# The same instructions in new fixed orders: five engine queues and the PSUM bank table of a two-layer transformer kernel laid out again

## The reference

```
x = layernorm(x + attention0(x))          # q, k, v, out without bias
x = layernorm(x + down0(silu(gate0(x) * gs) * (up0(x) * us)) * ds)      # 704 wide
x = layernorm(x + attention1(x))          # q, k, v, out with bias
x = layernorm(x + down1(silu(up1(x)) * gate1(x)))   # 1024 wide, weights made ternary
```

## Time and profile before

| | us |
|---|---|
| median of three runs | 256.35 (256.03 to 258.0) |
| the profiled execution, whole time | 255.42 |
| its span | 253.5 |
| PE, DVE busy | 240.6 (95%), 204.3 (81%) |
| ACT, POOL busy | 161.4 (64%), 167.1 (66%) |

### The profile page before, as it was taken

The page is one execution under the profiler, slowest core; times in us unless marked ns, Lnnn a source line. Parts: engine busy times, 40 slices in busy tenths (PEclk is TensorE's granted clock), DMA queues, the critical chain, the costliest instruction groups (busy, mean ns, idle before and its releaser), DMA issues.

```text
span 253.5 us, 6724 instructions
## 1 busy us (share of the span) xinstructions
PE 240.6 (95%) x2398; PEld 216.3 (85%) x2398; DVE 204.3 (81%) x599; ACT 161.4 (64%) x290; POOL 167.1 (66%) x218
## 2 busy tenths in 40 slices
PE   8998989999999999999999898998999999999991
PEld 8997967877789989989999897765788888999990
DVE  2477976999776876889999998998999975767664
ACT  4682465469889979627444567848788484555551
...
GB/s 164 277 193 203 216 175 241 152 120 79 76 98 109 109 129 119 85 145 144 187 85 189 3 122 189 31 153 145 0 45 3 4 3 0 3 35 8 3 0 124
DMA packets 23312, 26.39 MB, mean 104 GB/s; under 512 B 3184, under 2 KB 18288, under 8 KB 23280
## 3 DMA queue, kind: packets, MB, share of 16 engines
...
## 4 chain that ended last, share of the span: by engine, by line
PE 71%; POOL 6%; DVE 5%; DMA 5%; ACT 5%; issue 4%; SPq 2%; POOLq 0%; ACTq 0%
PE psum L566 9%; PE psum L567 8%; PE psum L568 8%; PE psum L686 6%; PE psum L661 5%; PE psum L741 5%; PE psum L742 5%; DMA k_stack<-k_part 3%; PE psum L629 3%; PE psum L689 2%; PE psum L633 2%; PE psum L664 2%; POOL hidden L1253 2%; PE psum L775 2%; PE psum L638 2%
## 5 line engine op out<-in xcount | busy, mean ns | idle before, releaser
L857 ACT ACTIVATE probs<-psum 128x768 f32<-128x768 f32 x64 | 49.1, 809 | 11.9 <-PE psum L667 5.9
L1253 POOL TENSOR_TENSOR hidden<-hf,hidden 128x512 fp32r<-128x512 f32 x24 | 31.6, 1320 | 13.5 <-ACT hidden L899 13.5
L1221 POOL TENSOR_SCALAR_AFFINE_SELECT probs<-probs 128x512 f32<-128x512 f32 x48 | 32.3, 688 | 10.1 <-ACT probs L857 9.7
L1009 DVE TENSOR_REDUCE block_max<-psum 128x6 f32<-128x768 f32 x32 | 28.9, 946 | 6.0 <-PE psum L633 5.9
L661 PE MATMUL psum<-q_stack,k_stack 98*128 98x256 bf16 x128 | 28.6, 274 | 2.1 <-DMA q_stack<-maxT_lo 1.0
L1020 DVE CUSTOM_DVE_ANT_0 masked<-psum,mask 128x256 bf16<-128x256 f32 x64 | 26.7, 418 | 1.6 <-issue 0.9
L1106 DVE SCALAR_TENSOR_TENSOR hf<-th,psum 128x512 f32<-128x512 f32 x28 | 18.9, 677 | 9.8 <-ACT th L888 3.9
L566 PE MATMUL psum<-xT_hi,gu_hi 128*128 128x256 f32 x88 | 25.3, 288 | 0.0
L567 PE MATMUL psum<-xT_lo,gu_hi 128*128 128x256 f32 x88 | 24.9, 283 | 0.0
L568 PE MATMUL psum<-xT_hi,gu_lo 128*128 128x256 f32 x88 | 24.9, 283 | 0.0
L664 PE MATMUL psum<-q_stack,k_stack 98*128 98x128 bf16 x128 | 24.7, 218 | 0.0
...
## 6 DMA issues: line engine op xcount, KB each, us to landing
q_stack<-q_part SPq DMA_DIRECT2D x48, 128.0 KB, 2.7
k_stack<-k_part SPq DMA_DIRECT2D x48, 128.0 KB, 2.4
...
```

Source lines behind the costliest of these rows:

```text
L857: nc.scalar.activation(probs[(n - 1) % 4][:, :, :], place(key)[:, :, 0:T + P], ACT.Exp, scale=SC).then_inc(exp_done, 1)
L1009: nc.vector.tensor_reduce(block_max[b % 2][:, 2 * i:2 * i + 2, 1:4], both(key)[:, :, 0:3 * P].rearrange("p j (c t) -> p j c t", t=P), mybi ...
L1221: pool.affine_select(out=diag, in_=diag, compare_op=ALU.is_ge, fill=0.0, base=0, pattern=[[0, 2], [0, 2], [1, P]], channel_multiplier=-1). ...
L1253: pool.tensor_tensor(hidden[(n - 1) % NHID][1][:, :, :], hf[n % 2][:, :].rearrange("p (a t) -> p a t", a=2), hidden[(n - 1) % NHID][0][:, ...
```

## The change

The program of every engine consists of the same steps with the same code; only the six tables are different. One line of two of them:

```diff
@@ SYNC_STEPS, first line
-    LOAD:001 LOAD:003 QK:000 LOAD:002 QK:001 MID:000-1 LO:000-1 QK:010 MID:010 LO:010 MID:011 QK:011 LO:011 LO:020
+    LOAD:001 LOAD:003 LOAD:002 QK:000 MID:000 QK:001 MID:001 LO:000-1 LO:010 QK:010-1 MID:010-1 LO:011 LO:020-1
@@ TENSOR_STEPS, first line
-    QK:000 XI:010 QK:001 QK:010 XI:020 XI:030 QK:011 QK:020-1 V:000 V:010 S:000-4 QK:030 S:005-7 QK:031 S:010 MX:000
+    QK:000 XI:010 QK:001 QK:010 XI:020 XI:030 QK:011 QK:020-1 V:000 S:000 V:010 S:001-5 QK:030 S:006-7 QK:031 S:010
```

More of the change, by code:

```diff
@@ L101 @@
[L101 to L105, removed]
@@ new lines @@
+    S:000-7 MB:000 QK:030 S:010 MX:000 QK:031 S:011-5 SCALES:000 UT:000 IV:000 S:016-7 S:020 MB:010 S:021 UT:001
+    MX:010 YM:000 IV:001 S:022-7 YM:001 MB:020 YB:000 S:030 PREP0:004-5 MX:020 UT:010 S:031-2 PREP0:006 O:000 S:033
+    IV:010 UT:011 S:034 IV:011 S:035-7 MB:030 YM:010 XT:000 YM:011 UT:020 YB:010 MX:030 GU:000 IV:020 UT:021 YM:020
+    IV:021 YM:021 O:010 YB:020 GU:001-2 UT:030 HL:002 IV:030 O:020 XT:010 D:000 UT:031 IV:031 YM:030-1 TS:100 YB:030
+    GU:010-1 O:030 XT:020 XT:100 TERN:100 GU:012 TERN:101 QK:100 HL:012 TS:101 XT:030 TERN:102 D:010 TERN:103
@@ new lines @@
+    GU:020-1 TERN:104 QK:101 XT:110 TERN:105 GU:022 GU:030 HL:022 QK:110 S:100-1 TERN:106 QK:111 GU:031 S:102-3
+    D:020 S:104-5 GU:032 S:106-7 S:110 XT:120 HL:032 S:111-2 QK:120 MX:100 D:030 S:113 QK:121 CB:100 S:114-6 XT:130
+    TS:102 S:117 TERN:107 QK:130 MX:110 S:120 QK:131 UT:100 S:121-6 UT:101 IV:100 S:127 IV:101 YM:100-1 TERN:108
+    YB:100 UT:110 MX:120 S:130-2 O:100 S:133 UT:111 S:134-6 XT:200 TERN:109 S:137 IV:110-1 YM:110-1 MX:130 YB:110
+    GU:100 UT:120-1 IV:120 GU:101 O:110 IV:121 YM:120 TERN:1010-11 YM:121 UT:130 YB:120 GU:102-3 XT:210 O:120
@@ L139 @@
+    GU:110-1 UT:131 XT:220 IV:130-1 YM:130-1 YB:130 GU:112-3 D:100 O:130 GU:120 D:110 XT:230 GU:121-3 GU:130-3 D:120
+    DT:130-1 NT:130-1
 """
 GPSIMD_STEPS = """
-    SPLIT:000 VONES:000 SPLIT:001 SPLIT:010-1 SPLIT:020-1 SPLIT:030-1 PREP0:000-3 YT:000 PREP0:004-5 LN:000
-    PREP0:006 ST:020-3 PREP1:000 ST:024-7 PREP1:001-2 YT:010 HI:000 ST:030-3 LN:010 YT:020 ST:034 HI:001-2 ST:035-7
-    LN:020 LN:100 YT:030 HI:010 TERN:100 LN:030 TERN:101 HI:011 TERN:102 HI:012 SPLIT:100 TERN:103 LN:110 TERN:104-5
@@ new lines @@
+    PREP0:004-5 LN:000 ST:020-3 PREP0:006 PREP1:000-1 ST:024-7 YT:010 PREP1:002 ST:030-3 LN:010 HI:000 YT:020
+    HI:001-2 ST:034-7 LN:020 LN:100 YT:030 HI:010 TERN:100 LN:030 TERN:101 HI:011-2 TERN:102-3 SPLIT:100 LN:110
+    TERN:104 HI:020 TERN:105 SPLIT:101 HI:021 TERN:106-7 HI:022 HI:030 SPLIT:110-1 LN:120 HI:031 PREP1:003 HI:032
+    LN:130 SPLIT:120-1 ST:100-1 XC:100 XC:110 ST:102-7 TERN:108 SPLIT:130-1 ST:110-5 YT:100 TERN:109 ST:116-7 ST:120
+    LN:200 ST:121-5 TERN:1010 ST:126-7 YT:110 TERN:1011 ST:130-1 HI:100 ST:132-3 XC:120 LN:210 HI:101 YT:120
@@ L150 @@
 SYNC_STEPS = """
-    LOAD:001 LOAD:003 QK:000 LOAD:002 QK:001 MID:000-1 LO:000-1 QK:010 MID:010 LO:010 MID:011 QK:011 LO:011 LO:020
-    RAW:000-1 LOAD:000 MX:000 ML:000 LO:021 QK:020 MID:020-1 QK:021 RAW:002-3 MID:030 QK:030 MX:010 ML:010 MID:031
-    LO:030-1 QK:031 RAW:004-5 ML:020 MX:020 RAW:006-9 MX:030 ML:030 RAW:0010-25 QK:100 RAW:0026-27 MID:100 QK:101
-    MID:101 LO:100-1 RAW:0028-29 QK:110 RAW:0030 LO:110 QK:111 MID:110-1 LO:111 MX:100 ML:100 QK:120-1 MID:120-1
-    LO:120-1 RAW:0031-32 ML:110 MID:130 MX:110 MID:131 QK:130 LO:130 QK:131 LO:131 ML:120 MX:120 RAW:0033-34 MX:130
-    ML:130 LN:300 LN:310 LN:320 LT:130-1
+    LOAD:001 LOAD:003 LOAD:002 QK:000 MID:000 QK:001 MID:001 LO:000-1 LO:010 QK:010-1 MID:010-1 LO:011 LO:020-1
+    RAW:000 LOAD:000 RAW:001 MX:000 ML:000 MID:020-1 QK:020-1 RAW:002-3 QK:030 MID:030-1 MX:010 ML:010 QK:031
+    LO:030-1 RAW:004-6 ML:020 MX:020 RAW:007-10 MX:030 ML:030 RAW:0011-26 MID:100 RAW:0027 LO:100 QK:100-1 MID:101
+    LO:101 RAW:0028-30 QK:110-1 MID:110-1 LO:110-1 QK:120 ML:100 QK:121 MX:100 MID:120-1 LO:120-1 ML:110 RAW:0031
+    MX:110 RAW:0032 QK:130-1 MID:130-1 LO:130-1 ML:120 MX:120 RAW:0033-34 MX:130 ML:130 LN:300 LN:310 LN:320
+    LT:130-1
 """
 BANKS = """
[7 rows of a table removed]
[7 rows of a table added]
 """
```

65 lines of the change are left out of this document (28 added, 37 removed), and 14 rows, old and new, of the table BANKS.

## The result

| | before | after |
|---|---|---|
| median, same chip, four runs each | 256.19 us (255.89 to 258.0) | 259.58 us (257.9 to 260.03) |
| ratio, 95% interval | | 1.015 (1.011 to 1.019) |
| the profiled execution, its span | 255.42, 253.5 | 260.03, 258.1 |
| PE, DVE busy | 240.6, 204.3 | 240.9, 206.8 |

The change makes the kernel slower by 3.4 us, against a forecast of 2.9 us faster.

A forecast was written before the change was run, and what follows sets the result against it. The PE bounds the kernel, held up mostly by late transfers, with DVE a second bound from 124 us. Terms 1.3 + 0.9 + 0.8 - 0.1 = 2.9 us take 255.42 to 252.5, median 253.4 us; range 251.3 to 256.4.

The forecast's parts named there:

- Start: To 44 us: earlier copies and loads on SP, S:014 ahead of ST:000; gain 1.3 us, ends 0.3 and 1.7.
- 0.65 us of SP's queue: Start: LOAD:002 ahead of QK:000 on SP makes every later copy come 0.65 us earlier.
- 2.4 to land: Start: batch 0's last copy lands 2.4 us after its issue, so S:000 can start between 18 and 19.2.
- rival 2: SP's order is worth nothing; only the moved S step and POOL gain, 1.5 us: 254.9 us, chance 0.08.
- POOL's hidden part: 108 to 124 us: HI:012 ahead of TERN:102 ends D:012's wait; gain 0.9 us, ends 0 and 1.1.
- Layer 1's attention: 124 to 202 us: S:110's wait goes to about nothing, two DVE gaps close; gain 0.8 us.
- rival 4: RAW:0030 blocks the stacks if TERN:106 ends later on DVE, and MX:100 holds ST:100: 259 us, chance 0.06.
- Stages that are full: 44 to 108 and 202 to 244 us: steps too early cost; net -0.1 us, ends -1.5 and +0.4.
- put at nothing: After 176 us on POOL: XC:120 moves in, a HI and two ST steps go out ahead of LN:210; no effect.
- Rival 5: Transfers differ from those the orders were laid out with; wins in one place are lost elsewhere: 256.3 us, chance 0.07.
- signs of being wrong: 44 to 108 us has more than 0.5 us idle, or SP's RAW:0030 is issued later than 129.
- signs of being right: x load before 8 us, last copy by 16.7, ST:000 by 32.3, no L1248 wait, no DVE gaps, PE idle about 4.

The follow-up runs named there:

- d1: Kernel before with S:000 ahead of V:010 on the PE, nothing else: 258.35 us against 256.27, ratio 1.008.
- c1: Kernel before with LOAD:002 moved ahead of QK:000 on SP alone: 255.76 us against 256.03, ratio 0.999.
- d2: Kernel before with the changed kernel's first 28 steps of SP, nothing else: 258.36 us against 256.27, ratio 1.007.
- c3: Kernel before with HI:012 ahead of TERN:102 (POOL) and GU:020 (ACT), TERN:102 behind XT:030 on DVE: 257.18 us against 256.03, ratio 1.004.
- d4: Before's tables to 141 us, the changed kernel's behind, with XT:220 behind YB:130 and XC:130 behind YT:130 again: 255.47 us against 256.27, 0.998.
- b1: Changed kernel with XT:220 behind YB:130 on DVE and XC:130 behind YT:130 on POOL again: 259.05 us against before's 255.81, ratio 1.013.
- f2: d4 with XC:120 moved behind HI:101 on POOL: 255.03 us against before's 255.88, ratio 0.997.
- b4: Changed kernel with the edits of b1 and b3 and k's path to S:100 given way on four engines: 260.57 us, ratio 1.020 to before.
- f1: Changed kernel with V:010 ahead of S:000, before's orders in 90 to 141 us, XT:220 and XC:130 put back: 258.19 us against before's 255.88, 1.008.
- c2: Changed kernel with V:010 ahead of S:000 again on the PE, nothing else: 260.31 us, ratio 1.014 to before.
- d3: Changed kernel with V:010 ahead of S:000 and before's first 28 steps of SP: 258.85 us, ratio 1.012 to before.
- a1: Before's tables up to about 44 us, the changed kernel's from there on, banks dealt out anew: 257.76 us against before's 255.96, ratio 1.007.
- a2: Before's tables up to about 90 us, the changed kernel's from there on, banks dealt out anew: 258.47 us against before's 255.96, ratio 1.010.
- b3: Changed kernel with DVE's MX:020 ahead of S:030 and UT:010 ahead of PREP0:004-5, as before: 260.19 us, ratio 1.017 to before.

## Why the prediction was wrong

- **Start, +1.3 forecast, -1.3 measured.** The failed step is the sentence that the PE "comes to S:000 one V step earlier", so that "the wait is about as long as before". V:010 was the work that hid that wait. Behind S:000 it costs its 1.4 us, since S:000 starts when k's last part has landed, and at times the clock too (d1, +2.1 us in the median). So the maxima were not issued at 29.7 but at 30.86, and they took 3.3 us to land, not 2.3: ST:000 started at 34.2 instead of 32.0. The other step, that 0.65 us of SP's queue is 0.65 us of landing, fell with c1: the earlier trace rows show a queue without a pause, but the row on the DMA engines (share 0.74 over the stage) had to be read for the first 20 us. The "2.4 to land" of the earlier trace rows is a median over the run; here it was 4.2. The rule of the Trainium skill (DMA: Bandwidth & Descriptors, Anatomy of one DMA), which was rival 2, gives c1's result for its single step, but the trace doesn't agree with a fixed 2.0 us: the same copy took 2.49 us to land before and 3.63 in c1. And d2, where SP's whole order at the start cost 0.7%, speaks against rival 2.
- **POOL's hidden part, +0.9 forecast.** Right at its place: c3 shows 0.8 us at D:012. It didn't last. What was moved back on POOL (TERN:102, SPLIT:100) feeds DVE and k's stack copies at QK:110 and S:100. The changed kernel lost some 1 us at S:100 (0.94 shown), which the prediction never looked at. All seven profiles with the changed orders there idle at S:100, 0.55 to 1.51 us; of the nine with before's orders eight idle 0.04 us or less and one, d4, 1.07. From D:001 to XT:120 the two together cost 0.1.
- **Layer 1's attention, +0.8 forecast.** The DVE gaps did close, and the stage from XT:120 to GU:102 is 0.4 us shorter in the mean of 14 profiles, the term's right part. The wait at S:110 did not go to nothing (0.77 us shown): TERN:106 ended at 133.0, so RAW:0030 and twelve copies behind it slipped, the mechanism of rival 4. (Its reason was misread: HL:022 and S:101 stand ahead of TERN:106 in before's table too.) It cost nothing new, as the same wait was there before.
- **Stages that are full, -0.1 forecast, -2.8 measured** in the profiles (1.9, some 1 by the medians, and 0.9). This is the largest error. "Nothing to gain, only to lose" was said and then priced at almost nothing, without following the moved steps there: MX:020 behind PREP0:004-5 and RAW:006 ahead of ML:020, XT:220 ahead of IV:130, XC:130 ahead of YT:130. All four stand in the tables of the two kernels and could be read there; that the last two cost 1.1 us is shown by b1, the first two are only read from waits. At LN:210 the tables were misread: the two ST steps do not go out from ahead of it but come in with XC:120, and HI:101 goes behind it. That was "put at nothing"; D:101 waits 0.48 us for HI:101 in the changed kernel, and moving XC:120 (f2) ends it.
- **The rivals.** Rival 4's 259 us is near, for another reason. Rival 5, that the transfers differ from those that the orders were laid out with, is a part of what happened in the first two stages (ST:030's transfer), and its price of nothing was wrong. Both of the forecast's signs of being wrong are there, 2.09 us idle in 44 to 108 and RAW:0030 behind 129, and 10.5 us of PE idle in 0 to 202 instead of 4. Some of its signs of being right are there too, and show how little they prove: the x load at 6.74, the last copy out at 15.33, no wait for L1248, the two DVE gaps closed.

Shown by an edit of their own are the end (b1, b4, d4, f1), V:010 (d1), SP's start (d2), the zero of LOAD:002 (c1) and HI:012 (c3). V:010 and SP's start are shown from before's side alone: undone in the changed kernel (c2 1.014, d3 1.012, against 1.015) they win nothing that the medians can tell. That 44 to 90 us costs 1.9 us is what 17 profiles say and the medians in part (1.0 us by f1, nothing by a1 and a2); which of its moves does it is only read from waits, and the one edit tried there (b3) moved the wait on. The same holds for S:100. Not tried: both kernels with a bank table as the single difference.
